# Attention and expert layer: the output projection in float32r parts, a piece's low part laid over the whole one, the last batch's projection and norm placed earlier

## The reference

```
qk = x @ W_attn + b_attn;  q, k = halves of qk;  v = x         (16 heads of 16 channels)
y  = causal_softmax(q k^T / 4) v
e  = v[1:] - y[:-1];  k2 = x[:-1] @ W_k2 + b_k2;  q2 = q[1:]
y2 = causal_softmax(q2 k2^T / 4) e, with a zero row in front
x  = layernorm(x + (y @ W_proj + b_proj) + (y2 @ W_proj + b_proj))
x  = layernorm(x + ffn(x))
```

## Time and profile before

| | us |
|---|---|
| median of 3 executions | 2408.53 |
| lowest, highest | 2407.89, 2410.39 |
| profiled execution | 2417.51 |
| its span | 2415.4 |
| TensorE clock granted, mean share | 0.978 |

### The profile page before, as it was taken

The page is one execution under the profiler, slowest core; times in us unless marked ns, Lnnn a source line. Parts: engine busy times, 40 slices in busy tenths (PEclk is TensorE's granted clock), DMA queues, the critical chain, the costliest instruction groups (busy, mean ns, idle before and its releaser), DMA issues.

```text
span 2415.4 us, 64954 instructions
## 1 busy us (share of the span) xinstructions
PE 2319.0 (96%) x19670; PEld 1327.7 (55%) x19670; DVE 2089.4 (87%) x9242; ACT 1778.4 (74%) x3392; POOL 1523.3 (63%) x2375
## 2 busy tenths in 40 slices
PE   6999999999999999999999999999999999999996
PEld 4555555555555555555555555555555555555454
DVE  5889998899899989999899889999998899998554
ACT  3677777777777777777777777777777777777642
POOL 4466666766766666666666666666666667665432
PEclk7799999999999999999999999999999999999997
DMA  7465555655556556565555665655556555554121
GB/s 122 90 109 105 103 99 98 118 113 112 115 104 112 97 103 123 111 114 112 103 107 101 108 118 111 118 111 108 104 95 117 112 113 117 110 97 81 55 70 35
DMA packets 187732, 250.82 MB, mean 104 GB/s; under 512 B 26744, under 2 KB 103168, under 8 KB 187392
## 3 DMA queue, kind: packets, MB, share of 16 engines
q1 hardware_dynamic: 186432, 245.10, 53.6%
q10 hardware_dynamic: 960, 1.57, 0.5%
HBM read 74.60 MB, written 16.78 MB: 38 GB/s over the span
## 4 chain that ended last, share of the span: by engine, by line
PE 72%; ACT 12%; issue 6%; POOL 4%; DVE 3%; DMA 2%; SPq 1%; ACTq 0%; DVEq 0%; POOLq 0%
PE out_t L643 22%; PE score_t L682 18%; PE misc L734 11%; PE score L693 7%; ACT heads_t L567 5%; PE out_t L708 4%; PE misc L776 4%; ACT prob L541 4%; PE score L835 2%; DVE junk L899 2%; DMA stack_q<-neg_l 1%; POOL prob L437 1%; ACT resid L276 1%; PE misc L760 1%; SPq L374 1%
## 5 line engine op out<-in xcount | busy, mean ns | idle before, releaser
L899 DVE CUSTOM_DVE_ANT_0 junk<-score,mask_rows 128x384 bf16<-128x384 f32 (+3 forms) x3584 | 1686.6, 515 | 224.8 <-PE score L693 215.8
L541 ACT ACTIVATE prob<-score_t 128x512 f32<-128x512 f32 x2560 | 1368.4, 599 | 276.4 <-PE score_t L682 275.5
L437 POOL TENSOR_SCALAR_AFFINE_SELECT prob<-prob 128x512 f32<-128x512 f32 (+1 forms) x1280 | 710.5, 560 | 729.7 <-ACT prob L541 717.9
L682 PE MATMUL score_t<-stack_q,stack_k 50*128 50x128 f32 (+5 forms) x4096 | 985.2, 359 | 25.8 <-ACT prob L541 7.5
L693 PE MATMUL score<-stack_k,stack_q 48*128 48x512 f32 (+3 forms) x4096 | 982.5, 348 | 2.7 <-DVE max_cols L899 1.1
L682 PEld LDWEIGHTS score_t<-stack_q,stack_k 50*128 50x128 f32 (+1 forms) x4096 | 611.8, 186 | 565.6 <-ACT prob L541 304.1
L643 PE MATMUL out_t<-prob,value 128*17 128x512 f32 (+3 forms) x8192 | 658.0, 439 | 0.0
L693 PEld LDWEIGHTS score<-stack_k,stack_q 48*128 48x128 f32 x4096 | 618.4, 188 | 24.8 <-DVE max_cols L899 9.9
L899 DVE DVE_READ_ACCUMULATOR2_ANT max_cols<- 128x1 f32 x4096 | 339.5, 83 | 0.0
L643 PEld LDWEIGHTS out_t<-prob,value 128*17 128x17 f32 x8192 | 184.7, 97 | 211.1 <-issue 129.6
L459 POOL TENSOR_TENSOR part_l<-part_f,part_h 128x512 fp32r<-128x512 f32 x192 | 245.4, 1278 | 16.3
(11 more groups left out here) (99 smaller groups left out, 1703.0 us busy)
## 6 DMA issues: line engine op xcount, KB each, us to landing
stack_k<-part_h SPq DMA_DIRECT2D x512, 128.0 KB, 4.5
stack_k<-part_l SPq DMA_DIRECT2D x256, 128.0 KB, 5.1
stack_q<-part_h SPq DMA_DIRECT2D x248, 128.0 KB, 4.2
x_full<-x_turned SPq DMA_DIRECT2D x32, 512.0 KB, 13.1
x_in<-L_attn_x SPq DMA_DIRECT2D x32, 512.0 KB, 14.5
resid<-L_attn_x SPq DMA_DIRECT2D x32, 512.0 KB, 5.2
stack_q<-part_l SPq DMA_DIRECT2D x124, 128.0 KB, 5.1
layer_out<-resid SPq DMA_DIRECT2D x31, 512.0 KB, 7.6
```

The costliest lines, as they stand in the source:

```text
L437: e.affine_select(out=view, in_=view, compare_op=ALU.is_ge, fill=0.0, base=-unit_parts(unit)[1], pattern=[[0, runs], [0, cut], [1, P]], ch ...
L541: e.activation(prob[pair % RING][:, slot % 2 * 512:slot % 2 * 512 + 512], score_t[time % KEY_DEPTH][:, :], ACT.Exp, scale=1.0 / np.sqrt(HE ...
L682: done = e.matmul(score_t[now % KEY_DEPTH][:, col:col + n], keys[rows, pair, kb * P:(kb + 1) * P], stack_q[b % 2][rows, pair, kb * P:token ...
L899: e.tensor_tensor_reduce(junk[count % JUNK][:, 0:n], score[number % MAX_DEPTH][:, col:col + n], mask, 1.0, -3e38, ALU.add, ALU.max, max_co ...
```

## The change

1. The projection's operands become float32r parts: `wp_full` is split by POOL into `wp` high and low once, at the start (at (5,2) ahead of batch 0; `wp_full` lies over `prob3`, so ACT's first exponential waits for the split). ACT writes y twice, to `y_t[HIGH]` and to `heads_t`, and POOL subtracts them into `y_t[LOW]` at (1,5) and (2,5). ACT's next write of `heads_t` waits for that subtraction. PE does three matmuls in the place of each one.
2. `part_l` is laid over `part_f`, and `y_second` has one buffer in place of two. ACT's copy of piece n now waits for the DMAs of piece n - 2, and POOL doesn't; DVE's write of `y_second` waits for POOL's add of the group before.
3. Times of projection, statistics and norm are tables (`USUAL`, `LAST`). `USUAL` has the same times as before. For the last batch the second projection comes at place 4 in place of 6, the statistics at places 4 and 5, the norm at places 5 and 6, the store at (6,1).
4. The experts' final statistics are taken on DVE pair by pair with the last expert's updates, and the final store is two transfers.

```diff
-STATS_AT = ((5, 5), (6, 4), (7, 5), (0, 1))
-APPLY_AT = ((0, 7), (0, 9), (1, 1), (1, 3))
+USUAL = {"proj": ((3, 7), (6, 7)), "added": ((4, 0), (7, 0)), "stats": ((5, 5), (6, 4), (7, 5), (8, 1)),
+         "var": ((8, 3),), "guess": ((8, 4),), "refine": ((8, 5),), "apply": ((8, 7), (8, 9), (9, 1), (9, 3)), "store": ((9, 5),)}
+LAST = {"proj": ((3, 7), (4, 7)), "added": ((3, 9), (4, 9)), "stats": ((4, 1), (4, 3), (5, 1), (5, 2)),
+        "var": ((5, 3),), "guess": ((5, 4),), "refine": ((5, 5),), "apply": ((5, 7), (5, 8), (5, 9), (6, 0)), "store": ((6, 1),)}
...
-        wp = sb("wp", [P, halves, width])
+        wp = [sb(f"wp_{part}", [P, halves, width], F32R) for part in "hl"]
+        wp_full = nc.alloc_sbuf_tensor_at("wp_full", [P, halves, width], F32, offset=prob_at + 3 * pairs * tokens)
...
-        y_second = [sb(f"y_second{i}", [P, blocks, GROUP, HEAD_DIM]) for i in range(2)]
-        y_t = sb("y_t", [P, halves, tokens])
+        y_second = sb("y_second", [P, blocks, GROUP, HEAD_DIM])
+        y_t = [sb(f"y_t_{part}", [P, halves, tokens], F32R) for part in "hl"]
...
-        part_l = [sb(f"part_l{i}", [P, tokens], F32R) for i in range(2)]
+        part_l = [part[:, :].bitcast(F32R) for part in part_f]
...
+        def due(what, time):
+            for b in range(max(0, time // SLOTS // UNITS - 2), min(batches, time // SLOTS // UNITS)):
+                for n, (u, slot) in enumerate((LAST if b == batches - 1 else USUAL)[what]):
+                    if time == SLOTS * (UNITS * (b + 1) + u) + slot:
+                        return b, n
+            return None
...
 SP:
-            e.wait_ge(s_apply, blocks * NORMS)
-            e.dma_start(out[0].rearrange("(t p) c -> p t c", p=P), result).then_inc(s_out, 16)
+            for pair in range(2):
+                rows2 = slice(2 * pair, 2 * pair + 2)
+                e.wait_ge(s_apply, blocks * (NORMS - 1) + 2 * pair + 2)
+                e.dma_start(out[0].rearrange("(t p) c -> p t c", p=P)[:, rows2, :], result[:, rows2, :]).then_inc(s_out, 16)
...
 POOL:
                     e.wait_ge(s_full, n + 1)
-                    if n >= 2:
-                        was, was_hf = [v[:2] for v in PIECES.values() if v[2] == (n - 2) % N_PIECES][0]
-                        e.wait_ge(s_stack[was, was_hf], 16 * TERMS * SIDES * ((n - 2) // N_PIECES + 1))
                     e.tensor_copy(part_h[i][:, :], part_f[i][:, :]).then_inc(s_split, 1)
...
+                for hf in range(halves):
+                    if (place, slot) == ((1, 5), (2, 5))[hf] and 0 <= ahead - 1 < batches:
+                        e.wait_ge(s_yt, halves * (ahead - 1) + hf + 1)
+                        e.tensor_tensor(y_t[LOW][:, hf, :], heads_t[:, :], y_t[HIGH][:, hf, :].bitcast(F32), ALU.subtract).then_inc(s_ysplit, 1)
...
 ACT:
                     if n >= 2:
-                        e.wait_ge(s_split, 2 * (n - 1))
+                        was, was_hf = [v[:2] for v in PIECES.values() if v[2] == (n - 2) % N_PIECES][0]
+                        e.wait_ge(s_stack[was, was_hf], 16 * TERMS * SIDES * ((n - 2) // N_PIECES + 1))
                     e.activation(part_f[n % 2][:, :], misc[:, :], ACT.Identity, bias=bias_qk[:, column:column + 1]).then_inc(s_full, 1)
...
+                    if place in (2, 3) and ahead >= 1:
+                        e.wait_ge(s_ysplit, halves * (ahead - 1) + place - 1)
                     e.activation(heads_t[:, :], out_t[:, :], ACT.Identity, bias=sum_floor[:, 0:1]).then_inc(s_heads, 1)
...
-                        e.activation(y_t[:, hf, :], misc[:, :], ACT.Copy).then_inc(s_yt, 1)
+                        e.wait_ge(s_turned, min(unit, end))
+                        e.activation(y_t[HIGH][:, hf, :], misc[:, :], ACT.Copy)
+                        e.activation(heads_t[:, :], misc[:, :], ACT.Copy).then_inc(s_yt, 1)
...
 PE:
-                                for c in range(halves):
-                                    done = e.matmul(misc[:, j * width:(j + 1) * width], y_t[:, c, t * P:(t + 1) * P], wp[:, c, :],
-                                                    start=(c == 0), stop=(c == halves - 1))
+                        for c in range(halves):
+                            for i, (py, pw) in enumerate(zip(PARTS_Q, PARTS_K)):
+                                done = e.matmul(misc[:, j * width:(j + 1) * width], y_t[py][:, c, t * P:(t + 1) * P], wp[pw][:, c, :],
+                                                start=(c == 0 and i == 0), stop=(c == halves - 1 and i == TERMS - 1))
...
 DVE:
-                    if a and unit - 1 >= GROUPS + 2:
-                        e.wait_ge(s_added, GROUPS * b + g - 1)
+                    if a and unit - 1 >= GROUPS + 1:
+                        e.wait_ge(s_added, GROUPS * b + g)
...
+                    if ex == experts - 1:
+                        for t in (2 * pair, 2 * pair + 1):
+                            e.wait_ge(s_facc, 4 * ex + t + 1)
+                            take_stats(e, NORMS - 1, t, ffn)
```

More of the change, by code:

```diff
@@ L375, in _ @@
                                             tile[32 * side:32 * (side + 1), :].bitcast(F32)).then_inc(s_maxrow[a], 16)
-                b = ahead - 2
-                if (place, slot) == (1, 5) and 1 <= b < batches:
+                now_due = due("store", time)
+                if now_due and now_due[0]:
+                    b = now_due[0]
                     e.wait_ge(s_apply, blocks * (b + 1))
@@ L495, in _ @@
                             e.wait_ge(s_value2, GROUPS * (b + 1))
-                        e.tensor_tensor(y, y, y_second[g % 2][:, :, :, :], ALU.add).then_inc(s_added, 1)
+                        e.tensor_tensor(y, y, y_second[:, :, :, :], ALU.add).then_inc(s_added, 1)
                     else:
@@ L504, in _ @@
                                         ALU.subtract).then_inc(s_value2, 1)
-                b = ahead - 2
-                if (place, slot) == (0, 3) and 0 <= b < batches:
+                now_due = due("var", time)
+                if now_due:
+                    b = now_due[0]
                     e.wait_ge(s_aggr, b + 1)
@@ L511, in _ @@
                                     ALU.mult, ALU.add).then_inc(s_ln, 1)
-                if (place, slot) == (0, 5) and 0 <= b < batches:
-                    refine(e, b)
+                now_due = due("refine", time)
+                if now_due:
+                    refine(e, now_due[0])
                 made = up_of(time - 2)
@@ L930, in _ @@
-                b = ahead - 1
-                if 0 <= b < batches:
-                    for pair in range(2):
-                        if (place, slot) == ((4, 0), (7, 0))[pair]:
-                            rows2 = resid[:, 2 * pair:2 * pair + 2, :]
-                            e.wait_ge(s_proj, 2 * b + pair + 1)
-                            if pair == 0:
-                                e.wait_ge(s_biased, b + 1)
-                            e.tensor_tensor(rows2, misc[:, :].rearrange("p (t c) -> p t c", t=2), rows2, ALU.add).then_inc(s_attended, 1)
@@ L939, in _ @@
-                for t, at in enumerate(STATS_AT):
-                    b = ahead - (1 if at[0] else 2)
-                    if (place, slot) == at and 0 <= b < batches:
-                        if t % 2 == 0:
-                            e.wait_ge(s_attended, 2 * b + t // 2 + 1)
-                        take_stats(e, b, t, resid)
-                        if t == last:
-                            aggregate(e, b)
+                    e.tensor_tensor(y_second[:, :, :, :] if a else y, heads[:, :, :, 0:HEAD_DIM], wide, ALU.mult).then_inc(s_normal, 1)
@@ new lines, in _ @@
+                now_due = due("added", time)
+                if now_due:
+                    b, pair = now_due
+                    rows2 = resid[:, 2 * pair:2 * pair + 2, :]
+                    e.wait_ge(s_proj, 2 * b + pair + 1)
+                    if pair == 0:
+                        e.wait_ge(s_biased, b + 1)
+                    e.tensor_tensor(rows2, misc[:, :].rearrange("p (t c) -> p t c", t=2), rows2, ALU.add).then_inc(s_attended, 1)
+                now_due = due("stats", time)
+                if now_due:
+                    b, t = now_due
+                    if t % 2 == 0:
+                        e.wait_ge(s_attended, 2 * b + t // 2 + 1)
+                    take_stats(e, b, t, resid)
+                    if t == last:
+                        aggregate(e, b)
@@ L1005, in _ @@
                     e.tensor_tensor(inner[ex % 2][:, fb, :], lift[n % 2], sigm[n % 2], ALU.mult).then_inc(s_finner, 1)
-            e.wait_ge(s_facc, 4 * experts)
-            for t in range(blocks):
-                take_stats(e, NORMS - 1, t, ffn)
             aggregate(e, NORMS - 1)
```

59 lines of the change are left out of this document (32 added, 27 removed).

## The result

| | before | after |
|---|---|---|
| median of the runs, us | 2409.46 (2407.89 to 2415.7, 4 runs) | 2500.11 (2491.95 to 2507.97, 4 runs) |
| profiled execution, us (span) | 2417.5 (2415.4) | 2502.65 (2500.8) |
| mean granted clock of TensorE | 0.978 | 0.975 |

After / before is 1.0374, 95% interval 1.0347 to 1.040: slower by 91 us. The forecast was 2435, 26 slower, with a range from 2406 to 2454. The direction was right and the size was not.

The account below looks back on a forecast made before the run. PE in its written order sets the pace. Loss 42 + 5.3 against gain 8.7 + 5.7 + 4 made 29 us slower on the profiled execution, taken as 27 for timed runs: 2435 us, range 2406 to 2454.

Parts of the forecast that it names:

- places 1 and 2: wait and y copies: Second and third of a batch's eight units: ACT's landing wait loses 42 us, the second y copy 5.3.
- place 3: Fourth of a batch's eight units: 0.18 us of the projection's gain lands on the mean, times 31, 5.7 us.
- place 6: Seventh of a batch's eight units: 0.28 us of the projection's gain lands, times 31, 8.7 us.
- place 7: Eighth of a batch's eight units: no change counted; DVE's next full stretch lies there.
- behind the steady part: Tail after the last down matmuls: 6.3 us gained, about 2.3 lost to the moved projection; net 4, between 1 and 7.
- ahead of it: Prologue: the weights' split falls where POOL stands for ACT, so it costs nothing.
- The deciding term: ACT's second k piece copy waits for the first k piece's landing: 1.4 us per batch, 42 in all, bounds 10 and 60.
- PE delay is the wait less 0.4: In a batch's third unit, PE's third score is late by ACT's wait less 0.4: 1.90 us in one batch.
- My upper bound of 2.0 us a batch: POOL's mask, piece split and value subtraction pass lateness on: 60 us in place of 42, 2453, chance 0.10.
- The y copies: ACT's second y copy delays PE 0.33 us in the second unit (inside the wait), 0.17 in the third; 5.3 in all.
- The projection: A pair of blocks becomes 12 matmuls at 0.117 us, 1.40 against 1.73: a gain of 0.32 us per pair.
- that rival: The projection's weight loads are not hidden: 61 us lost where 14 was gained, 2510 us, chance 0.05.

Follow-up runs that it names:

- spread: The changed kernel with the 127-row load of x_next cut in two loads of 112 and 15 rows: 2411.67 us.
- pool: The changed kernel with one y copy on ACT, into heads_t, and POOL making the high part; 127-row load uncut: 2503.32 us.
- before_low: The kernel before with only part_l laid on part_f, ACT instead of POOL waiting for the landing of piece n-2: 2474.98 us.
- dose6: The changed kernel with the 127-row load cut in two and six extra ACT copies of the second k piece to part_f: 2588.78 us.
- wpend: The changed kernel with the projection weights' low part allocated last, so other tensors keep the SBUF addresses of the kernel before: 2494.35 us.
- before_low_pad: before_low with an unused tensor of 2 KB per partition ahead of the stacks, giving the changed kernel's addresses behind it: 2476.68 us.
- before_low_single: before_low with y_second as one buffer as well: 2468.87 us.
- spread_pool: The changed kernel with the 127-row load cut in two, one y copy on ACT into heads_t, and POOL making the high part: 2396.94 us.
- before_spread: The kernel before with the 127-row load of x_next cut in two loads of 112 and 15 rows: 2407.96 us.
- dose3: The changed kernel with the 127-row load cut in two and three extra ACT copies of the second k piece to part_f: 2476.26 us.

## Why the prediction was right and wrong, step by step

| step | forecast, us | measured, us |
|---|---|---|
| places 1 and 2: wait and y copies | +47 | +107 (30 x 3.56) |
| place 3 | -5.7 | -13 (30 x 0.43) |
| place 6 | -8.7 | -8 (30 x 0.27) |
| place 7 | 0 | +4 (30 x 0.12) |
| behind the steady part | -4 | -11 |
| ahead of it | 0 | +7 |

**The deciding term: right mechanism, too small.** ACT waits for the first k piece, in every batch, where and why the prediction said; spread removes that one cause and with it 88 of the 91 us. The step that failed is the size of this term, 30 x 1.4 = 42 with an upper bound of 60. Of the 107 us of places 1 and 2 the second y copy of place 2 is about 7 (30 x 0.23, by pool), which leaves 100 for it. It was too small in two ways, of which the second is the larger.
First, "PE delay is the wait less 0.4", added up as if PE ran on at its old speed. That rule holds at full clock: before_low, which has the forecast's premises, gives 46 us against my 42. What I left out is that behind such a stand the clock can be at 0.50. That is 17 us in before_low and 12 x (9.74 - 8.11) = 20 in the changed kernel. The page of before shows the clock below 0.9 only in its first two slices and its last, and I took full clock in the steady part as given, though my own change made the stand that ends it. The trace of before has one such stretch in the steady part, 6.8 us long, in the last place of the last of these batches, behind a window in which PE was busy for 0.66 us of 1.60:
```profile
2221.00:2222.60 1.60, 0.66 (x9) 0.39 (x6) 1.57 (x9) 1.44 (x3) 0.73 (x2) 1.00 0.09 21
2224.00:2226.00 2.00, 2.00 (x12) 0.24 (x10) 1.55 (x10) 0.60 (x1) 0.95 (x2) 0.50 0.65 198
```
I did not look for it. The Trainium skill (TensorE: Matmul & The Clock Gate, Part 1) says that the array's clock falls back to its lower level when TensorE has been idle; by it this should have been a term of the sum. The runs agree: in dose6, where no DMA is waited for, every batch has it, at 1.7 us each.
Second, I read the landing times off the trace of before and kept them. In the changed kernel the piece lands at 10.88 in place of 9.61, while its last transfer is issued 0.16 later: 1.27 x 30 = 38 us. What is left, 107 - 20 - 38 = 49, is what the forecast had as 47. The lateness as a whole is the 127-row load's, which is shown. Why it is 1.3 us worse in this family of kernels is open: not the addresses, not `y_second`, not ACT's copies, which were tried. The new projection, the split of its weights and the rest of the new program were not tried singly. The traces show where it arises: `x_in` is issued 9.3 us ahead of place 1 as before (9.4) and lands at 6.9 in place of 4.8, and the 1 KB packets in the first two microseconds of place 1 last 137 to 139 ns on the mean in after, wpend and pool, against 121 to 128 in before, before_low, before_low_pad and before_low_single. So the packets of the straggling engine are slower; what makes them so, no run shows.
My upper bound of 2.0 us a batch came from a mechanism (POOL passing lateness on) for which the trace has no place: place 2 follows from ACT's wait alone, within 0.01 us.

**The y copies: right.** 0.33 late in place 1 and 0.17 in place 2 were forecast; spread, which has no wait in their way, shows 0.41 and 0.24 against spread_pool. That the first lies inside the wait is shown by pool.

**The projection: right.** A pair's records in place 6, first and last of twelve:
```profile
1084.23 0.39 PE L810 MATMUL misc<-wp_h,y_t_h 128*128 128x256 f32 x1
1084.46 0.28 PE L810 MATMUL misc<-wp_l,y_t_h 128*128 128x256 f32 x1
1084.58 0.28 PE L810 MATMUL misc<-wp_h,y_t_l 128*128 128x256 f32 x1
...
1085.64 0.28 PE L810 MATMUL misc<-wp_h,y_t_l 128*128 128x256 f32 x1
```
The steps are 0.117, but for a first of 0.23, beside the earlier trace rows. The weight loads (0.19 us each, one per matmul) keep the same step and add nothing to it, so that rival is out. (The prediction's 0.107 for a load and 1.31 for a pair are not quite what rows 5 give, 0.11 and 1.32; nothing hangs on that.) Place 6 gave its 0.27. Place 7 took 0.12 of it back: PE's turning of the maxima now waits for DVE for 15.7 us in 37 waits, where it was 3.0 in 7. So places 6 and 7 together gave 0.15 a batch, and not the 0.28 of the forecast.
**Place 3** gave 0.43, more than the pair's gain. In the kernel before two batches have a place 3 of over 10 us (10.58 and 10.13), and after none is over 9.1. In before_spread, too, the mean is 8.95 in place of 9.10. So part of this is the scatter of the `neg_l` wait and not the change.

**Ends.** The last down matmuls end at 2491.65 and the span at 2500.8:
```profile
2487.85 3.80 PE score L884 x8
2491.67 0.87 DVE ffn L1023 x2
2492.79 0.42 DVE stats L320
```
That is 9.2 us where it was 16.4, 7.2 shorter against 6.3 forecast. From the start of the last place to the end it is 97.3 us; the kernels without the new ending have 100.9 to 105.3, so its net gain is 3.6 to 8. The 7 us ahead of the steady part are the same wait a 31st time, in the batch before it, where the forecast had none. Place 2 of that batch lasts 14.6 us against 8.2 before, and its rows are
```profile
89.87 0.69 ACT L582 ACTIVATE part_f<-misc,bias_qk 128x512 f32<-128x512 f32 x1 [3.10 <-DMA stack_k<-part_f]
```
```profile
93.00:95.00 2.00, 2.00 (x18) 0.84 (x8) 0.34 (x1) 1.06 (x2) 2.00 (x3) 0.50 0.30 96
```
That is 6.4 of the 7 us. The split of the weights adds nothing that shows: the whole stretch is 142.5 to 145.0 us in five of the six other kernels that have it (dose6 has 153.0, with 13.7 in this place), against 139.4 to 145.3 in the five without it. wpend and pool have the 31st wait too, with 11.9 and 10.5 us in this place; the rest of the stretch varies by a few us with where in it the clock is low.

**Sum.** Against the forecast of 29 on the profiled execution: +38 for the later landing, +20 for the clock, +4 for place 7, +7 for the wait ahead of the steady part, +2 in the rest of places 1 and 2, +1 for place 6, -7 for place 3 and -7 behind: 87 comes out, beside the spans' 85.

## What to carry to other kernels

A wait moved to an engine on the path must be priced with the landing's scatter and with what PE's stand does to its clock: in before_low 46 us of delay cost 63. A buffer is cheap to share where its landing is early, so look first at what delays the landing. One load of 127 rows held the 512 KB loads and the piece behind it back by 7 to 9 us; cutting it in 112 and 15 rows freed the change from its price, and with a copy moved to the engine that has slack the kernel is 0.7% faster than before.
When one delay lies inside another, removing the inner one alone shows nothing: the same y edit was worth 15 us with the load split and nothing without.

## What the hardware showed that was not expected

- In one batch a stand of PE of 2.56 us was followed by the clock at 0.50, in which 24 matmuls took 2.76 us for 1.49; in another a stand of 1.65 was not. Batches of the changed kernel with ACT waiting 2.4 to 3.5 us are found on both sides; the six with more all had it, and so had all 30 of dose6.
- Of 16 counts of one load, 15 came within 7.9 us and the last at 16.1.
- The same 1 KB packets last 137 to 139 ns in three kernels and 121 to 128 in four others, with the same DMAs.
- `resid`'s load takes 5.9 to 6.1 us in the changed kernel, spread, spread_pool, wpend and pool, and 5.1 to 5.3 in those built on the kernel before, but also 5.1 in dose3 and 3.9 in dose6. No run explained either.
